# The attention stage's loop over pairs of images, written out

## The reference: a conv block, attention with relative positions, and a mixture of experts

```python
x = x + _L0_conv_ref(_gn(x), ...)                 # depthwise convs, FFNs, window attention
t = _to_tokens(x)                                 # 16 x 1024 tokens x 128 channels
t = t + _L1_attn_ref(_ln_t(t), ...)
t = t + _L1_ffn_ref(_ln_t(t), ...)                # 8 experts, the best 2 of each token

# _L1_attn_ref, 4 heads of 32 channels:
content_score = jnp.einsum('bshd,bthd->bhst', q + u_bias, k)
pos_score = rel_shift(jnp.einsum('bshd,thd->bhst', q + v_bias, p))
attn = jax.nn.softmax((content_score + pos_score) / np.sqrt(D), axis=-1)
ctx = jnp.einsum('bhst,bthd->bshd', attn, v).reshape(B, S, D)
return ctx @ Wout + bout
```

## Time and profile before

| | us |
|---|---|
| median of three runs | 4112.44 (4105.55 to 4118.47) |
| the profiled execution: its own time | 4110.17 |
| its span | 4107.7 |
| PE busy | 3243.4 (79%) |
| DVE busy | 2720.2 (66%) |
| ACT busy | 2203.8 (54%) |
| POOL busy | 745.2 (18%) |
| mean granted TensorE clock | 0.88 of full speed |

### The profile page before, as it was taken

The page is one execution under the profiler, slowest core; times in us unless marked ns, Lnnn a source line. Parts: engine busy times, 40 slices in busy tenths (PEclk is TensorE's granted clock), DMA queues, the critical chain, the costliest instruction groups (busy, mean ns, idle before and its releaser), DMA issues. The chain is left out here.

```text
span 4107.7 us, 80297 instructions
## 1 busy us (share of the span) xinstructions
PE 3243.4 (79%) x29652; PEld 2491.6 (61%) x29652; DVE 2720.2 (66%) x5162; ACT 2203.8 (54%) x3568; POOL 745.2 (18%) x869
## 2 busy tenths in 40 slices
PE   4789888987565888787887787878877885699993
PEld 2555655665453666666666665667666764587772
DVE  4877787776443767666766676667666764477773
ACT  2545555554453656555655565556655653477770
POOL 1000000000111020212021202120212112466660
PEclk9999999998777988888998898888888987799995
DMA  2544554454587999888988898889888983477768
GB/s 54 162 121 155 177 158 125 159 172 141 213 306 245 364 332 321 296 298 303 326 318 281 302 332 301 293 292 326 318 283 302 336 302 134 165 238 238 244 207 328
DMA packets 291011, 1023.87 MB, mean 249 GB/s; under 512 B 51620, under 2 KB 57520, under 8 KB 281574
## 3 DMA queue, kind: packets, MB, share of 16 engines
q1 hardware_dynamic: 273382, 985.62, 69.7%
q0 software_dynamic: 17280, 33.87, 2.3%
HBM read 486.25 MB, written 489.85 MB: 238 GB/s over the span
## 5 line engine op out<-in xcount | busy, mean ns | idle before, releaser
L1089 DVE CUSTOM_DVE_ANT_0 att_skewed<-att_score_ps,att_skewed 128x1024 f32<-128x1024 f32 x512 | 625.5, 1222 | 325.5 <-issue 303.9
L951 ACT ACTIVATE att_skewed<-att_skewed,att_neg_max 128x1024 f32<-128x1024 f32 x512 | 588.8, 1150 | 369.1 <-DVE att_neg_max L1089 332.9
L942 ACT ACTIVATE att_rows<-att_wide_ps 128x1152 f32<-128x1152 f32 x512 | 573.8, 1121 | 371.0 <-PE att_wide_ps L1171 282.9
L1097 DVE COPY att_turned<-att_turn_ps 128x1024 f32<-128x1024 f32 x512 | 625.4, 1222 | 148.1 <-remote 109.0
L1207 PE MATMUL att_turn_ps<-att_ident,att_skewed 128*128 128x128 f32 x4096 | 598.1, 293 | 119.1 <-ACT att_skewed L951 93.9
L1207 PEld LDWEIGHTS att_turn_ps<-att_ident,att_skewed 128*128 128x128 f32 x4096 | 499.5, 150 | 290.4 <-ACT att_skewed L951 218.6
L1171 PE MATMUL att_wide_ps<-att_ps,att_qs 98*128 98x128 f32 (+3 forms) x1920 | 455.7, 360 | 44.0 <-ACT att_rows L942 19.0
L1217 PE MATMUL att_tail_ps<-att_turned,att_vals 128*32 128x128 f32 x8192 | 320.1, 288 | 125.9 <-issue 124.2
L1199 PE MATMUL att_score_ps<-att_ks,att_qs 96*128 96x512 f32 x1024 | 385.3, 460 | 15.4 <-DVE att_neg_max L1089 14.1
L906 POOL DMA_INDIRECT expert_rows<-att_expert_rows,att_place x256 | 247.1, 965 | 787.8 <-DVE att_place L1047 702.0
L1171 PEld LDWEIGHTS att_wide_ps<-att_ps,att_qs 98*128 98x128 f32 x1920 | 324.3, 209 | 104.4 <-issue 49.0
(11 more groups left out here) (256 smaller groups left out, 5301.9 us busy)
## 6 DMA issues: line engine op xcount, KB each, us to landing
skewed_rows<-att_rows SPq DMA_DIRECT2D x512, 576.0 KB
att_skewed<-skewed_rows SPq DMA_DIRECT2D x512, 512.0 KB, 6.2
expert_rows<-conv_pad SPq DMA_DIRECT2D x144, 520.0 KB, 10.9
exp_weights<-split_weights SPq DMA_DIRECT2D x71, 1028.0 KB
att_qs<-queries SPq DMA_DIRECT2D x192, 128.0 KB
att_ks<-keys SPq DMA_DIRECT2D x192, 128.0 KB
exp_rows<-expert_rows SPq DMA_DIRECT2D x71, 260.0 KB
sum_part<-expert_parts SPq DMA_DIRECT2D x32, 512.0 KB, 8.6
```

What stands on the lines that cost most here:

```text
L942: act.activation(rows[s % ROWS][:], wide_ps[:, 0:WIDE], ACT.Copy).then_inc(wide_read, 1)
L951: act.activation(skewed[r % RING][:], skewed[r % RING][:], ACT.Exp, bias=neg_max[:, k:k + 1], scale=-1.0, accum_out=sums[:, k:k + 1]).then ...
L1089: dve.tensor_tensor_reduce(skewed[r % RING][:], score_ps[:], skewed[r % RING][:], -SCALE, 3.0e38, ALU.add, ALU.min, neg_max[:, k:k + 1]).t ...
L1097: dve.tensor_copy(turned[r % (2 * HEADS)][:], turn_ps[:]).then_inc(turn_read, 1)
```

## The change: images 1 to 14 are called with plain numbers

```diff
--- before.py
+++ after.py
@@ -762,11 +762,8 @@
                 for s in range(STEPS):
                     slot(n, b, s)
 
-            image(0, 0)
-            with eng.Fori(0, (NB - 2) // 2) as pair:
-                image(2 * pair + 1, 1)
-                image(2 * pair + 2, 0)
-            image(NB - 1, 1)
+            for n in range(NB):
+                image(n, n % 2)
             for s in range(STEPS, STEPS + ROUTE_END):
                 slot(NB - 1, 1, s)
```

## The result

The changed kernel took 4092.39 us, the median of six runs (4082.4 to 4095.66); the kernel before took 4110.25 beside it (4105.55 to 4118.47, six runs). The ratio is 0.9949, interval 0.9933 to 0.9965. So it is faster, clear of the noise but by far less than 2%: the medians differ by 18 us where 36 were forecast. The profiled execution of the changed kernel took 4082.40, the lowest of the six, 10 us under the median; the forecast of 4074 was made against a profiled execution too. The gain is therefore 0.5 to 0.7%, 20 to 30 us.

A forecast was written before the change was run, and what follows sets the result against it. The attention stage was taken as bound by a chain of hand-overs, broken by the loop's jumps. Savings of 18.3 + 5.1 + 13.0 = 36.4 us from the profiled 4110.2 gave 4073.8, said as 4074; range 4054 to 4096.

The forecast's parts named there:

- Bound by hand-overs: Attention stage: no engine is full; a chain of hand-overs between engines, broken by something that comes back, sets the time.
- Part 1: Last slots of images 2, 4, 6, 8, 10 and 12: removing the six jumps back saves 18.3 us.
- Part 2: First 8 slots of the six images behind a jump: no restart at a lower granted clock, saving 5.1 us.
- Part 3: Waits in images 1 to 14: constants replace register operations, saving 0.93 us per image, 13.0 us in all.
- The price stands somewhere else: Rival, 0.07: the long last slot is the tail of the scatters, so only part 3 remains; 4097 us.
- GpSimd's gap: Rival, 0.07: constants bring GpSimd's long hold-up among the scatters to 13 more images, costing 40 us; 4114 us.
- Late instruction blocks: Rival, 0.04: in straight code instruction blocks come late, also among the scatters, making the kernel slower; 4130 us.
- More: Rival, 0.20: register work also costs 0.83 us in each image's second half, restart at its upper value; gain 47.4, 4063 us.

The follow-up runs named there:

- again: The changed kernel run once more with no edit; 4088.8 us, ratio 0.9926 to the kernel before.
- dve_loop: The changed kernel with the loop over image pairs left in place on VectorE alone; 4124.11 us, ratio 1.0003 to the kernel before.
- others_loop: The changed kernel with the loop over image pairs kept on all looping engines except VectorE; 4105.15 us, ratio 0.9966 to the kernel before.
- pe_loop: The changed kernel with the loop over image pairs left in place on TensorE alone; 4097.93 us, ratio 0.9946 to the kernel before.

## Why the prediction was right, and where its size was wrong

- *Bound by hand-overs, with the jumps as one link.* Right. DMA's share on the plateau is as before, and the gain of the jumps, of the restart and of slots 0 to 15 stands at the forecast places.
- *Part 1, 18.3 us.* Measured 18.1 (18.9 in `again`). The size was right and its explanation by TensorE's branch was not: that branch alone costs 5.7. ScalarE's own jump makes the last slot long (at image 8 TensorE's), and VectorE's, at the same time, would cost more in the slots behind. The earlier trace rows show standstills of three engines at once, and the one quoted as the proof was not the one on the path; the sum came out all the same, because it was read from the length of the slots, whichever engine's jump it is.
- *Part 2, 5.1 us.* Measured 4.2, and clock 1.00 behind every former jump but at image 9 (0.96).
- *Part 3, 13.0 us: the term that was mis-sized.* For slots 0 to 15 it took 0.83 per image; measured 0.74 to 0.89, 10 to 12 us in fourteen images, nearly all VectorE's. For slots 16 to 31 it took 0.1 more. Slots 24 to 31, the jumps apart, gave 2 to 4 us, and slots 16 to 23 lost 6.6 to 10.3. The step that failed is the sentence that waits for GpSimd cover register work, with 0 as the floor. The wait ended no sooner, so nothing could be won there, and TensorE's matmuls behind it ran at a lower clock in more images: slot 17 alone gave back 7.3 us. The floor should have been below nothing. Why the clock is lower there more often is not known. Part 3 came to 29.6 - 18.1 - 4.2 = 7.3 us in the changed kernel's trace, and to 26.6 - 18.9 - 4.2 = 3.5 in that of `again`, not 13.
- *The sum.* The images gave 29.6 us in the changed kernel's trace and 26.6 in `again`; the other 7 to 10 of the 36.4 were lost in slots 16 to 23. From there to the median are the phases outside: image 0, image 15 and all that follows took 2.5 us more in the profiled execution, 4.9 in `again`, and the median stands 10 above the profiled execution in the first set. That spread of ten was taken as six. The measured 4092 lies 4 us inside the upper end of the range, which had been set for parts 2 and 3 at nearly nothing. They gave 7.7 to 11.5 us and were not nothing; it was their shortfall and an unlucky distance between profiled execution and median together that brought the time there. The direction was earned, the place in the range is partly luck.
- *Rivals.* "The price stands somewhere else" (4097) lies nearer to the median than the forecast does, but its mechanism is refuted: the last slots fell to 3.4. GpSimd's gap stayed at images 8 and 15. Late instruction blocks: slots 0 to 15 take 50.6 us in the even images, as image 15 did before, so nothing of that size is exposed there, and in the kernel before TensorE's instruction packets took 1.06 us each in slots 26 to 30 and 1.01 elsewhere, so they are hardly slower among the scatters. "More" is refuted by slots 16 to 23.

## What to carry to other kernels

When all engines jump at once, their standstills overlap. A long branch row does not say that its engine is on the path, and a short one does not say that the jump was cheap: look at the sequencer's next operation behind the branch, and put the loop on one engine alone before crediting a price to it. Ask of each piece of saved time which wait it runs into: what VectorE gained in slots 0 to 15, 10 to 12 us, stayed there, and slots 16 to 23, with the wait for GpSimd's sixteenth operation in them, lost 6.6 to 10.3 us of it again. And the largest wait was no part of this change: pulling sixteen scatters apart gave 5.5% more, seven to eleven times what writing out the loop gave.

## What the runs showed of the hardware beyond what was expected

- Each engine pays for its own jump back: VectorE idles 3.13 to 3.55 us at five of the six jumps of `dve_loop`, ScalarE 3.07 at the first jump of `others_loop`, and TensorE's branch has a median of 3.53 in `pe_loop`. From branch to the sequencer's next operation it is 4.2 us on VectorE and 4.0 on ScalarE at these first jumps, though their branch rows are 68 and 45 ns long. What of it shows depends on how much handed-over work the engine still has: TensorE had enough of it at five of six jumps. A standstill of VectorE cost up to 5 us, where TensorE's granted clock was 0.89 over the next 8 slots.
- An idle time of TensorE of 3.10 us before slot 18 was followed by matmuls at full rate (0.82 us for four of L1171), one of 3.20 us by the same at 1.41 us. The granted clock of slot 17 was 0.97 and 0.77. It isn't the length of this idle time that decides: after 3.10 us they took 1.42 in `pe_loop`, after 3.24 us 0.82 in `dve_loop`. Both lengths of slot 17 come in both kernels, before has the longer one in five images and the changed kernel in twelve, and what decides between them stays open.
- Sixteen indirect DMAs issued every 1.26 us in slots 27 to 30 cost the rest of the core 14.8 us per image; the same sixteen in slots 27 to 40 cost little.
